# The down product between gate and val: a new order inside the feed-forward tiles of a gated block

## The reference

```python
def bit_linear(x, w, b):
    gamma_x = jnp.clip(jnp.max(jnp.abs(x), axis=-1, keepdims=True), 1e-05, None)
    scale_x = 127.0 / gamma_x
    x_dq = jnp.clip(jnp.round(x * scale_x), -128.0, 127.0) / scale_x
    ...
    gamma_w = jnp.clip(jnp.mean(jnp.abs(w)), 1e-05, None)
    w_dq = jnp.clip(jnp.round(w / gamma_w), -1.0, 1.0) * gamma_w
    ...
    return jnp.einsum('bsd,hd->bsh', x_ste, w_ste) + b
...
gate = jax.nn.silu(bit_linear(x, gate_w, gate_b))
val = bit_linear(x, val_w, val_b)
return bit_linear(gate * val, out_w, out_b)
```

## Time and profile before

| | us |
|---|---|
| median of 3 runs | 317.08 (316.98 to 319.25) |
| the profiled execution | 316.65 |
| span of its trace | 314.9 |
| TensorE busy | 293.4 (93% of the span) |
| VectorE busy | 262.5 (83%) |
| GpSimd busy | 236.7 (75%) |
| ScalarE busy | 214.4 (68%) |
| mean granted TensorE clock | 0.997 |

### The profile page before, as it was taken

How to read it: one execution, slowest core, us unless ns; L and a number is a source line. 1 busy time by engine, 2 the same in 40 slices (tenths; PEclk the granted TensorE clock), 3 DMA queues, 4 the chain that set the end, 5 groups by cost and what they waited for, 6 DMA issues and landing times.

```text
span 314.9 us, 5289 instructions
## 1 busy us (share of the span) xinstructions
PE 293.4 (93%) x1424; PEld 142.5 (45%) x1439; DVE 262.5 (83%) x499; ACT 214.4 (68%) x268; POOL 236.7 (75%) x260
## 2 busy tenths in 40 slices
PE   0979999999999999999889899999999999999981
PEld 0435555555555555544334344444444444444430
DVE  5869888868789986789998999998899889988850
ACT  4857688678866456786987788766976687664510
POOL 4554873798888779945776999898888987797722
PEclk9999999999999999999999999999999999999998
DMA  7689899674425822824152754546443542344171
GB/s 265 212 321 335 297 373 325 236 227 180 136 67 170 254 84 84 299 57 89 49 100 50 119 86 123 127 118 146 87 101 83 117 83 71 90 108 100 33 167 67
DMA packets 52549, 47.51 MB, mean 151 GB/s; under 512 B 44783, under 2 KB 44783, under 8 KB 50224
## 3 DMA queue, kind: packets, MB, share of 16 engines
q1 hardware_dynamic: 47968, 33.86, 39.6%
q0 software_dynamic: 4560, 13.40, 12.5%
HBM read 28.35 MB, written 10.00 MB: 122 GB/s over the span
## 4 chain that ended last, share of the span: by engine, by line
PE 82%; DVE 6%; DMA 5%; issue 2%; POOL 2%; ACT 1%; POOLq 0%; DVEq 0%
PE banks L585 31%; PE banks L652 16%; PE banks L661 16%; PE banks L676 14%; PE banks L592 3%; PE banks L562 2%; DMA raw<-in_ctx 2%; DVE raw L1117 1%; POOL w_both L443 1%; DMA out<-xg,raw 1%; DVE raw L1112 1%; DMA xg<-in_x,gather_at 1%; DVE xg L1142 1%; PE banks L548 1%; DMA tok<-in_itok_BxS 1%
## 5 line engine op out<-in xcount | busy, mean ns | idle before, releaser
L585 PE MATMUL banks<-w_both,turned 128*128 x444 | 102.0, 379 | 0.5 <-ACT turned L779 0.3
L443 POOL TENSOR_TENSOR w_both<-raw 128x1024 f32<-128x1024 f32 (+1 forms) x32 | 75.0, 2342 | 9.2 <-DVE raw L1112 7.2
L585 PEld LDWEIGHTS banks<-w_both,turned 128*128 128x128 f16 x444 | 43.4, 98 | 45.5 <-issue 1.6
L854 ACT ACTIVATE w_both<-w_both,magic,raw 128x1024 f32 (+1 forms) x31 | 38.2, 1234 | 36.4 <-DVE raw L1131 36.4
L676 PE MATMUL banks<-tern,xg 128*128 128x512 bf16 x248 | 59.6, 379 | 3.0 <-DVE xg L1142 1.0
L661 PE MATMUL banks<-tern,raw 128*128 128x512 bf16 x255 | 60.3, 379 | 1.3 <-DVE raw L1104 1.3
L652 PE MATMUL banks<-tern,raw 128*128 128x512 bf16 x251 | 59.9, 379 | 0.7 <-DVE raw L1112 0.4
L1104 DVE SCALAR_TENSOR_TENSOR raw<-banks,raw 128x1024 f32<-128x1024 f32 x32 | 40.9, 1278 | 5.7 <-issue 4.9
L1112 DVE SCALAR_TENSOR_TENSOR raw<-banks,raw 128x1024 f32<-128x1024 f32 x32 | 40.9, 1279 | 4.3 <-PE banks L661 4.3
L1117 DVE TENSOR_REDUCE raw<-w_both 128x1 f32<-128x1024 f32 x32 | 38.8, 1212 | 2.7 <-POOL w_both L443 2.6
L676 PEld LDWEIGHTS banks<-tern,xg 128*128 (+1 forms) x256 | 24.8, 98 | 33.7 <-DMA xg<-raw 1.8
(11 more groups left out here) (121 smaller groups left out, 397.5 us busy)
## 6 DMA issues: line engine op xcount, KB each, us to landing
raw<-in_ctx SPq DMA_DIRECT2D x4, 1024.0 KB, 6.5
raw<-in_L_ffn_gate_w SPq DMA_DIRECT2D x4, 1024.0 KB, 7.4
raw<-in_L_ffn_val_w SPq DMA_DIRECT2D x4, 1024.0 KB
raw<-in_L_ffn_out_w SPq DMA_DIRECT2D x4, 1024.0 KB, 5.2
raw<-x_low SPq DMA_DIRECT2D x8, 257.5 KB, 4.4
raw<-x_high SPq DMA_DIRECT2D x8, 257.5 KB, 4.1
raw<-in_L_ffn_gate_b SPq DMA_DIRECT2D x1, 1024.0 KB, 5.4
raw<-in_L_ffn_val_b SPq DMA_DIRECT2D x1, 1024.0 KB, 8.1
```

What stands on the lines that cost most here:

```text
L443: nc.gpsimd.tensor_tensor(z[:, t % 2, 2 * D * c:2 * D * c + width], g_sb[:, c, 0:width], v_sb[:, c, 0:width], ALU.mult).then_inc(z_made, 1)
L585: last = nc.tensor.matmul(acc[:, :], a[:, k * P:(k + 1) * P], flat(w[:, bass.ds(e4 + k, 1), :]), start=(k == 0 and i == 0), stop=(k == KD ...
L854: nc.scalar.activation(zq[:, a:b], flat(z[:, bass.ds(t % 2, 1), a:b]), ACT.Identity, scale=flat(sc[:, bass.ds(t, 1), 12:13]), bias=magic[: ...
```

## The change

In slots 3 to 14, each down group goes between gate and val: G0 D0 V0 G1 D1 V1 in place of G0 V0 D0 G1 V1 D1. Slot 15, and slots 0 to 2, stay. On VectorE, `finish(t - 3)` goes in front of `pre_val(t, 1)`, in slots 3 to 14.

```diff
-            def ffn_slot(t, third, downs=True, start_down=False):
+            def ffn_slot(t, third, downs=True, start_down=False, between=False):
 
                 pe.wait_ge(x_turned, 16 * (t + 1))
                 gate(t, 2 * t, 0, third)
+                if between:
+                    down(t - 3, 0, start_down)
                 val(t, 2 * t, 0, (third + 1) % 3)
-                if downs:
+                if downs and not between:
                     down(t - 3, 0, start_down)
                 gate(t, 2 * t + 1, 1, (third + 2) % 3)
+                if between:
+                    down(t - 3, 1)
                 val(t, 2 * t + 1, 1, third)
-                if downs:
+                if downs and not between:
                     down(t - 3, 1)
...
-            ffn_slot(3, 1, start_down=True)
+            ffn_slot(3, 1, start_down=True, between=True)
             with pe.Fori(0, 3) as r:
                 for n in range(3):
-                    ffn_slot(3 * r + n + 4, (n + 2) % 3)
-            ffn_slot(TILES - 3, 2)
-            ffn_slot(TILES - 2, 0)
+                    ffn_slot(3 * r + n + 4, (n + 2) % 3, between=True)
+            ffn_slot(TILES - 3, 2, between=True)
+            ffn_slot(TILES - 2, 0, between=True)
             ffn_slot(TILES - 1, 1)
...
                 if 1 <= t < TILES - 1:
                     z_max(t, 0)
+                if 3 <= t < TILES - 1:
+                    finish(t - 3)
                 pre_val(t, 1)
...
-                if 3 <= t < TILES - 1:
-                    finish(t - 3)
```

## The result

The change makes the kernel slower. The median was 324.58 us (322.17 to 326.7, 4 runs) against 318.13 before (4 runs), a ratio of 1.020 with an interval of 1.011 to 1.029. That it is slower is clear of the scatter; whether by a little less or a little more than 2% is not. The forecast was 322.1 with a range of 319.8 to 324.0: the sign, the place and the mechanism were right, the size was too small, and the first median lies 0.6 us outside the range (the second, 323.51, inside it).

A forecast was written before the change was run, and what follows sets the result against it. TensorE was taken to bound the kernel at 10.36 us per slot. Ten round trips of 10.81 from D0 of slot 4 at 173.33 made +5.04 us on 316.65, then 0.43 for the median: 322.1, range 319.8 to 324.0.

The forecast's parts named there:

- TensorE's floor of 10.36 us: Slots 5 to 14: TensorE's matmuls alone need 10.36 us per slot, six groups of 1.727 us.
- the slots that could only keep or lose: Slots 5 to 14: TensorE was busy 103.33 of 103.70 us, so a new order could gain nothing there.
- the ring: Closed loop of waits between TensorE and VectorE, D0 to next slot's D0: 10.81 us per slot, D0 waiting 0.45 us.
- first three legs: D0's start to V0's start 1.73 us, to V0's eviction 1.93, to finish 6.22.
- the way into it: Slots 3 and 4: D0 fills the pause before V0 of slot 3; D0 of slot 4 starts at 173.33.
- ten further round trips: From D0 of slot 4 at 173.33, ten times 10.81 us puts D0 of slot 14 at 281.43.
- ring waits: TensorE's gates waiting on v_made and vals on g_made, for PSUM banks to be evicted; counted as zero cost.
- Rival 1: D0 waits once, in slot 4, then finish keeps ahead; kernel not slower, 317.6 or 315.2 us; chance 0.08.
- rival 2: GpSimd's product to z comes late and z_max of half 0 waits in each slot; 327 us; chance 0.05.
- this sign of being wrong: The forecast is wrong if z_max at L1121 on VectorE shows idle time ended by GpSimd.
- Rival 3: Each pause brings one TensorE group to the lower 1.2 GHz clock, 1.73 us more per slot; 339 us; chance 0.02.
- the last leg, the way back: Finish's start on VectorE to the next slot's D0 on TensorE: 0.93 us, 0.19 of it behind finish's end.

The follow-up runs named there:

- e1: Changed kernel with finish(t - 3) one more step forward on VectorE, ahead of z_max(t, 0); ratio to the kernel before 1.000 (0.997 to 1.003).
- e2: Changed kernel with xn in SBUF, down sums alternating between two PSUM banks and the loop over slots 4 to 12 unrolled; ratio to the kernel before 0.996.
- e3: Changed kernel with TensorE's new order only in slots 3, 5, 8, 11 and 14, VectorE as changed; ratio to the kernel before 1.002.
- e11: Changed kernel, TensorE's wait for half 0's transposed z moved from D0 to the slot's start; G0 of slot 3 to G0 of slot 15 took 133.13 us.
- e5: Changed kernel with finish back in its old place behind pre_val(t, 1), so only TensorE's half is changed; ratio to the kernel before 1.063.
- e8: The changed kernel run again with no edit; median 323.51 us, ratio to the kernel before 1.021 (1.015 to 1.027).
- e4: Changed kernel with TensorE's loop over slots 4 to 12 written out; G0 of slot 3 to G0 of slot 15 took 131.12 us, one run.

## Why the prediction fell short

**What held.** TensorE's floor of 10.36 us; the slots that could only keep or lose; the ring and each of its first three legs (1.73, 1.93, 6.22 against 1.74, 1.93, 6.22); the way into it, slot 3's gain included; ten further round trips; GpSimd's products, transposes and ring waits off the path from slot 5 on (slots of 10.36 in e1 under the same order); the end unchanged. Rival 1, the open ring, is excluded by the changed trace. So is rival 2, GpSimd: the leg from V0's eviction to finish is still 6.22 us, and from slot 4 to slot 14 no z_max (L1121) has idle time that GpSimd ended. Ahead of that three have, of 0.17, 0.19 and 0.92 us, but the kernel before has the same three (and three more in slots 4 to 6), so this sign of being wrong does not speak against the ring. Rival 3, a lower clock behind each short pause, is excluded by the 1.00 of the window from 183 to 293 us. e1, e2 and e3 each break the ring at another place and each bring back 10.36 (e3 from slot 6 on).

**The step that failed: the last leg, the way back.** I took it from one row, 0.93 us, with bounds of 0.80 and 0.93 from two and only 0.05 added on top. The trace has 0.93 in the first copy of the loop's body, 1.03 in the second and third, and 0.88 to 0.89 in slots 13 and 14. My one row happened to be of the first copy. D0 of slot 4 to D0 of slot 14 took 284.58 - 175.86 = 108.72 us against 108.1, which is the 0.6 us between 5.65 and the 5.04 of the forecast. The upper bound was too tight: the order of instructions, which I had, shows different waits on the three copies. The estimate from the page of the Trainium skill (Advanced Engine Details and Errata, Miscellaneous Facts), 0.05 to 0.10 us to read a semaphore, gave 4.1 us for the sum and lies further off. The trace agrees with it only in e11's slots outside the loop, where D0 starts 0.05 us behind finish's end; in the changed kernel it is 0.14 to 0.30 us.

This step does not by itself carry the median out of the range: with 5.65 in place of 5.04 the forecast would have been 322.7. The first median is 2.5 us above 322.1. Of that 0.6 is this leg, 1.05 is the kernel before, whose median came out at 318.13 where I had 317.08 from three runs, and the last 0.8 is scatter and the clock, which four runs do not take apart.

**The second step: the clock.** I weighed only the repeated pause of 0.45 us. But my own numbers had TensorE at D0 of slot 4 by 171.0 and released at 173.33, a pause of more than 2 us, twice what the earlier trace rows had shown, and the earlier trace rows could not vouch for that. In the two profiled executions of the changed kernel the clock held at 1.00 through slot 4. Among its eight timed runs two stand out, 326.7 and 326.99 us at mean clocks of 0.988 and 0.987; the other six are at 0.993 or more, and the lowest of 70 runs of the kernel before has 0.991. e11's trace (mean clock 0.989) shows what such a spell costs, 1.7 us. That the two runs had it at the same place is likely from their clock and not seen, since they have no trace. The rule that I cited from the Trainium skill (TensorE: Matmul & The Clock Gate, "A second HAM failure mode: psum-queue depth-cycling", on micro-idles between groups) did not come true as it reads: ten pauses of 0.25 to 0.40 us, and in e5 ten of 1.4 to 1.6 us, left the slots even at a granted clock of 1.00. What was followed by a fall was one longer pause: of the four traced executions with 2.10 to 2.13 us at D0 of slot 4 (the changed kernel, e8, e4, e11) only e11 shows one, and why stays open.

**The rest is scatter.** The median before was 317.08 over three runs, 318.13 over four, and 317.6 to 317.9 over more than twenty, and the part ahead of slot 3 moves by up to 3.9 us between executions. My range put 0.05 us per slot on the upper side and gave that scatter hardly any room.

## What to carry to other kernels

When two engines hand the same buffer back and forth, add the legs of the round trip and compare the sum with the time per iteration; a wait that has 2 us of room in the old order can close a ring by moving one group, and idle time that lies outside the ring's legs does not help. To test for such a ring, break it at three different places (a shorter leg, a second buffer, every other iteration): if all three restore the pace, little but the ring is left. Price a leg from every copy of the code that will run, with the waits that each carries, and look for the one long pause as well as for the many short ones.

## What the hardware showed that I had not expected

- A semaphore wait costs TensorE's restart different amounts by the instruction that carries it. From finish's start to D0's start it is 1.03 us where the wait on `o_made` has a semaphore instruction of its own in front of the loop's address instruction, and 0.93 where the address instruction carries it. Outside the loop it is 0.88 to 0.89 with a semaphore instruction in front of the matmul, and 0.79 to 0.80 where the matmul carries the wait (e11).
- A single pause of 2.13 us was followed by a fall of the granted clock in one traced execution (e11) and by none in three others (the changed kernel and e8, and e4 with 2.10 us), with the pause at the same place. In e5, ten pauses of 1.4 to 1.6 us in ten slots were followed by none, and the one of 3.33 us ahead of them was.
